# One TensorE loop for all eight attention batches, and VectorE adding all four expert planes: a macaron block on one core

## What is computed

```python
x = x + 0.5 * ffn(layernorm(x))          # mixture of experts + shared expert
x = x + attention(layernorm(x))          # linear attention, causal, 16 heads of 8
x = x + 0.5 * ffn(layernorm(x))          # the same weights as the first

# ffn: scores = softmax(x @ gate_w.T); the top 6 of 64 experts (with gate_b added) take the token
#      y = sum over the 6 of weight * (silu(x @ w1.T) * (x @ w3.T)) @ w2.T   (at most 64 tokens an expert)
#      z = (silu(x @ ws1.T) * (x @ ws3.T)) @ ws2.T                            (every token)
# attention: q = elu(q) + 1, k = elu(k) + 1; out = q.(running sum of k v) / q.(running sum of k)
```

## Time and profile before

| | before |
|---|---|
| median of 3 runs | 602.3 us (601.03 to 602.94) |
| the profiled execution, its own time | 599.64 us |
| its span, first to last instruction | 597.7 us |
| TensorE busy / GpSimd / VectorE / ScalarE | 72% / 55% / 53% / 41% |
| mean granted TensorE clock | 0.716 of full |

### The profile page before, as it was taken

One profiled execution on the slowest core, in us unless ns is written; L12 is line 12 of the kernel. 1 busy time (PEld: TensorE's weight loads), 2 busy tenths in 40 slices (PEclk: granted clock), 3 DMA queues, 4 the chain that ended last, 5 costly groups with the idle time before them and its releaser, 6 DMA issues.

```text
span 597.7 us, 15203 instructions
## 1 busy us (share of the span) xinstructions
PE 427.4 (72%) x5988; PEld 280.2 (47%) x5988; DVE 316.6 (53%) x927; ACT 243.2 (41%) x637; POOL 331.5 (55%) x259
## 2 busy tenths in 40 slices
PE   1884969994689325667999987158676999558970
PEld 1842645552345213455777875156344555224440
DVE  6386982221113992445576763476999322112097
ACT  4872113331223358634577740098411333112420
POOL 6085777888886800311244320005977788887691
PEclk9988785555559855679899985558979555555975
DMA  8997700101008990000021111530000010100592
GB/s 256 379 260 293 286 9 9 10 5 10 6 5 302 409 408 5 0 4 21 18 53 41 48 36 39 202 153 15 0 1 10 7 10 4 10 6 6 202 395 105
DMA packets 34387, 60.38 MB, mean 101 GB/s; under 512 B 12611, under 2 KB 18846, under 8 KB 33870
## 3 DMA queue, kind: packets, MB, share of 16 engines
q1 hardware_dynamic: 23078, 58.41, 27.5%
q0 software_dynamic: 11264, 1.38, 2.6%
HBM read 37.43 MB, written 29.36 MB: 112 GB/s over the span
## 4 chain that ended last, share of the span: by engine, by line
PE 37%; DVE 28%; DMA 13%; issue 11%; POOL 5%; ACT 5%; SPq 1%; POOLq 0%; DVEq 0%; ACTq 0%
DVE X L976 9%; DMA rows_d<-A 5%; PE bank L777 5%; PE upper L877 5%; PE upper L794 4%; DVE Cb L1078 3%; DMA planes_d<-Bb,put_i 3%; ACT A L507 3%; POOL planes_d L438 3%; DVE bn L981 2%; POOL A L452 2%; DMA Bb<-planes_d 2%; PE bank L894 2%; PE upper L913 2%; PE bank L832 2%
## 5 line engine op out<-in xcount | busy, mean ns | idle before, releaser
L438 POOL DMA_INDIRECT planes_d<-Bb,put_i x64 | 100.4, 1569 | 21.5 <-issue 16.0
L479 POOL TENSOR_TENSOR Bb<-Cb,chm 128x576 f32<-128x576 f32 x32 | 36.9, 1183 | 110.3 <-PE upper L924 75.7
L452 POOL DMA_INDIRECT A<-rows_d,tok_i x64 | 71.9, 1124 | 20.6 <-issue 16.9
L1108 DVE TENSOR_TENSOR ring<-ring,bank 128x88 f32<-128x88 f32 x64 | 15.8, 246 | 101.1 <-ACT ring L575 101.1
L674 PE MATMUL bank<-ident,A 128*128 128x128 f32 x96 | 22.5, 412 | 56.4 <-ACT A L507 42.2
L396 POOL TENSOR_TENSOR Bb<-Eb,st 128x512 f32<-128x512 f32 x8 | 8.9, 1115 | 72.4 <-DVE st L1026 72.4
L674 PEld LDWEIGHTS bank<-ident,A 128*128 128x128 f32 x96 | 18.1, 220 | 59.3 <-issue 30.0
L794 PE MATMUL upper<-w2s,ring 88*64 88x128 f32 x256 | 44.0, 448 | 0.0
L1112 DVE TENSOR_SCALAR Bb<-upper,sl 128x128 f32<-128x128 f32 x64 | 22.5, 351 | 30.2 <-PE upper L794 30.0
L976 DVE TENSOR_TENSOR X<-X,A 128x1024 f32<-128x1024 f32 x8 | 18.5, 2318 | 33.9 <-DMA Bb<-planes_d 33.9
L777 PE MATMUL bank<-w1s,ring 128*64 128x88 f32 x256 | 35.6, 378 | 0.0
(11 more groups left out here) (171 smaller groups left out, 1071.3 us busy)
## 6 DMA issues: line engine op xcount, KB each, us to landing
planes_d<-zeros SPq DMA_DIRECT2D x8, 2048.0 KB, 20.7
w3s<-in_w3T SPq DMA_DIRECT2D x2, 2816.0 KB
rows_d<-A SPq DMA_DIRECT2D x8, 512.0 KB, 11.7
A<-planes_d SPq DMA_DIRECT2D x8, 512.0 KB, 9.1
PL<-planes_d SPq DMA_DIRECT2D x8, 512.0 KB, 9.8
Cb<-planes_d SPq DMA_DIRECT2D x8, 512.0 KB, 10.5
Bb<-planes_d SPq DMA_DIRECT2D x8, 512.0 KB, 11.3
w1s<-in_w1T SPq DMA_DIRECT2D x1, 2816.0 KB
```

What stands on the lines that cost most here:

```text
L438: pool.indirect_dma_start(out=planes_d[f], in_=Y[:, s, :], in_offset=None, out_offset=bass.IndirectOffsetOnAxis(ap=put_i[:, s:s + 1], axis=0),
L452: pool.indirect_dma_start(out=A[:, t, :], out_offset=None, in_=rows_d, in_offset=bass.IndirectOffsetOnAxis(ap=tok_i[:, t:t + 1], axis=0), ...
L479: pool.tensor_tensor(out=VX[:, :, :, c, :].rearrange("p q h f -> p (q h) f"), in0=VN.rearrange("p q h f -> p (q h) f"), in1=chm[:, c:c + 1 ...
```

## The change

There are two parts. In attention TensorE's hardware loop runs all eight batches, and no batch is written out. So batch 0 now also runs `turn_out(-1)` and `project_out(-1)` on what lies in the buffers, and batch 7 also runs `project(8)` and `turn_k(8)`; none of these results is used. ScalarE and VectorE raise semaphores in advance or at the end, so that these extra steps find their waits met; their own instructions are the same. In both tails `add_planes` and its semaphore go, and VectorE adds all four planes.

```diff
--- before.py
+++ after.py
@@ gpsimd
-                def add_planes(g):
-                    cols = slice(g * GI * D, (g + 1) * GI * D)
-                    pool.wait_ge(part_in[g], 16 + 64 * (f + 1))
-                    pool.tensor_tensor(out=PLANES[2][:, cols], in0=PLANES[2][:, cols], in1=PLANES[3][:, cols],
-                                       op=ALU.add).then_inc(planes_added, 1)
-
                 for g in range(EARLY, NSH):
-                    if g >= NSH - 2:
-                        add_planes(g - (NSH - 2))
                     shared_gates(g)
-                for g in range(2, NG):
-                    add_planes(g)
@@ scalar
+            act.sem_inc(anT_sb, PRIMED)
...
             def step(b, first=False, last=False):
-                if not last:
+                if last:
+                    act.sem_inc(q_read, 2)
+                    act.sem_inc(k_read, 2)
+                else:
                     features(b + 1)
-                    if not (isinstance(b, int) and b + 2 >= B):
+                    if isinstance(b, int) and b + 2 >= B:
+                        act.sem_inc(hTb_sb, 1)
+                    else:
                         slice_h(b + 2)
@@ tensor
-            for s in (v_ps, sc_ps, kv_ps, pr_ps, o_ps, anT_ps):
+            for s in (v_ps, sc_ps, kv_ps, o_ps):
                 pe.sem_inc(s, PRIMED)
...
-                pe.wait_ge(an_ready, b + 1)
+                pe.wait_ge(an_ready, PRIMED + b + 1)
...
-                pe.wait_ge(anT_sb, b + 1)
+                pe.wait_ge(anT_sb, PRIMED + b + 1)
...
-            def step(b, first=False, last=False):
-                if not last:
-                    project(b + 1)
+            def step(b):
+                project(b + 1)
                 pe.wait_ge(q4_ready, 4 * b + 4)
                 pe.wait_ge(k_ready, PRIMED + b + 1)
-                if not first:
-                    turn_out(b - 1)
+                turn_out(b - 1)
...
-                if not first:
-                    project_out(b - 1)
+                project_out(b - 1)
...
-                if not last:
-                    turn_k(b + 1)
+                turn_k(b + 1)
 
             project(0)
             turn_k(0)
-            step(0, first=True)
-            with pe.Fori(0, B - 2) as i:
-                step(i + 1)
-            step(B - 1, last=True)
+            with pe.Fori(0, B) as b:
+                step(b)
             turn_out(B - 1)
             project_out(B - 1)
@@ vector
-                    for buf in PLANES[0:3]:
-                        if buf is PLANES[2]:
-                            dve.wait_ge(planes_added, NG * (n // 2) + g + 1)
+                    for buf in PLANES:
                         then(dve.tensor_tensor(xg, xg, buf[:, cols], ALU.add))
...
-            for s in (q_ready, k_ready, kv_sb, oo_ready):
+            for s in (q_ready, k_ready, kv_sb, oo_ready, an_ready):
                 dve.sem_inc(s, PRIMED)
...
-                if not last:
+                if last:
+                    dve.sem_inc(k_ready, 1)
+                else:
                     k_feature(b + 1)
```

More of the change, by code:

```diff
@@ L226, in macaron_kernel @@
         z_added = sem("z_added")
-        planes_added = sem("planes_added")
         out_done = sem("out_done")
@@ L885, in step @@
                         pe.wait_ge(v_ready, b + 1)
-                        if not last:
-                            pe.wait_ge(q_read, 2 * (b + 2))
-                            pe.wait_ge(k_read, 2 * (b + 2))
+                        pe.wait_ge(q_read, 2 * (b + 2))
+                        pe.wait_ge(k_read, 2 * (b + 2))
                     for q in AFTER[g]:
@@ L1192, in step @@
                 dve.wait_ge(o_ps, PRIMED + b + 1)
-                if not first:
-                    dve.wait_ge(anT_ps, PRIMED + b)
+                dve.wait_ge(anT_ps, PRIMED + b)
                 ob = upper[:, :, 0:NC * GW].rearrange("p g (n f) -> p g n f", f=E + 1)
```

## The result

| | before | changed |
|---|---|---|
| median | 601.85 us (601.03 to 602.94, 4 runs) | 578.57 us (576.1 to 585.32, 4 runs) |
| ratio | | 0.9598, 95% interval 0.9551 to 0.9646 |
| profiled execution, own time and span | 599.64 and 597.7 us | 577.09 and 575.3 us |

One of the changed kernel's four runs, the one of 585.32, was in a slow state and is left out of the ratio but not of the median above; the median of the other three is 577.09. Five more rounds on another occasion gave 0.9608 (0.9583 to 0.9633). The median fell by 23.3 us (24.8 with the median of the three), where 20.4 were forecast.

What follows compares the result with a forecast made beforehand. No engine bounds the whole: TensorE bounds attention, slowed by code loading and idle time, and VectorE the tails, held by GpSimd. Gains 14.2 + 2.6 + 3.6 = 20.4 us from 602.3 give 581.9, range 577 to 590.

Steps and rivals of the forecast that it cites:

- Batch 0 in the loop: Attention's first pass: still loads code, 19.25 us, plus 1.0 (between 0 and 1.6) for the extra steps.
- Batch 1: Attention's second pass: finds its code in place, so takes 14.19 us like batch 2 before, instead of 19.02.
- batches 2 to 6: Attention's middle passes: 12.63 us each at the full clock, 63.15 together.
- Batch 7 and the end: Attention's last pass in the loop: full clock, no idle time, attention ending at about 361.3 instead of 375.49.
- the first rival: Attention: the clock stays low in batch 7, so attention gives 5.4 + 1.4; time 589.3, chance 0.1.
- a stall behind the loop: Attention's end: code behind the loop may be missing when the branch falls through, costing 0 to 2.8 us.
- the second: Tails give nothing: bunched gates hold VectorE as long as GpSimd's adds did; time 588.1, chance 0.1.
- the third: Attention: each loop pass loads its code again, batches 1 to 7 taking 19 us; time 625.3, chance 0.03.
- the fourth: Attention: code loading was not the issue time, stalls stay in batch 1; time 587.3, chance 0.1.
- The reason given for batch 7: Attention: straight code stops TensorE 1.62 us; 2.71 us idle before ScalarE's k copies brings the clock to 0.59.
- Packets of code: Instruction queue: the changed kernel's trace should show some four to five fewer code packets.
- The tails: Both tails: VectorE no longer held by GpSimd's adds, gaining 2.6 us in stage 0 and 3.6 in the last.

Runs made afterwards that it cites:

- last_straight_full: Changed kernel with TensorE's batch 7 as straight code behind a loop over seven batches, `project(8)` and `turn_k(8)` kept; ratio to before 0.9744.
- loop_only: Kernel before with only the attention loop change, both tails as before; ratio to before 0.9773, median 588.96 us.
- tails_only: Kernel before with only the change to both tails, attention as before; ratio to before 0.9849, median 595.01 us.
- the spare kernels: Changed kernel plus unused GpSimd adds, or memsets of the same size, at the old places; ratios to before 0.9912 and 0.9625.
- after_again: The changed kernel itself, run again as the measure on one chip; 580.29 us, ratio to before 0.9608.
- last_straight: Changed kernel with TensorE's batch 7 as straight code behind the loop, without `project(8)` and `turn_k(8)`; ratio to before 0.9735.
- unrolled: Changed kernel with all eight TensorE batches in straight code, no loop; 613.27 us, ratio to before 1.0262.
- plane_waits: Changed kernel with a semaphore for each plane of each column group; ratio to before 0.9574, and 0.9543 when run again.

## Why the prediction was right

The forecast was 581.9 us in 577 to 590, and 578.57 lies in it. By its own steps:

**Batch 0 in the loop**: 20.2 us forecast, 18.40 measured. I let the added 1.6 us of `turn_out(-1)` and `project_out(-1)` cost 1.0; the batch took 0.85 less than before in spite of them, so the good bound, that they are free, fits. It is not shown: the stretch varies from 17.98 to 19.33 us between the kernels with the loop, which is more than the term. That the extra work hides in the stops for code (0.58, 0.87 and 2.14 us) is the likely reason.

**Batch 1** 14.19 forecast, 14.67 measured; **batches 2 to 6** 63.15 forecast, 63.17 measured. **Batch 7 and the end** 16.1 forecast, 16.48 measured. So attention gave 15.2 where 14.2 stood in the sum. The low clock in batch 7 (the first rival) did not come, nor a stall behind the loop, nor tails that give nothing (the second), nor reloading on each pass (the third), nor stalls left in batch 1 (the fourth).

**The reason given for batch 7** was right in its parts and wrong in their weights. The prediction spoke of a second trouble, the idle 2.71 us and the low clock behind it, and named it beside a stop of 1.62 us for code, as if the larger part were the clock. `last_straight_full` shows the clock kept up and only 1.2 us gained: the two causes overlap, since at the low clock TensorE takes up the time in which it would otherwise wait for code. The change removed both at once, and the sum took batch 7 whole from batch 6, so it did not need the weights and came out right. (The price of the first rival is about 1 us too low: 16.7 - 1.6 + 3 + 5.5 is 23.6 already without the "one more us" for `turn_k(8)`.)

**Packets of code**: "four to five fewer" was wrong, it was eight (27 to 19). I counted one copy of a batch; the change takes away two. `loop_only` has 19 too, and `tails_only` 27.

**The tails**: 2.6 and 3.6 forecast, 4.0 and 5.0 measured. The mechanism and the price of an add (1.22 to 1.23) were right; a gate took 1.26 to 1.40 us by itself, where 1.42 stood. The term mis-sized was the time in which gates hold VectorE. I took 2.8 and 4.2 us. Measured, from the adds above 1.23 us, it is (2.03 - 1.22) + (2.18 - 1.22) = 1.8 in the tail of stage 0, where the last gate ran beside the statistics. In the last tail three adds are held, and not one for a gate's full 1.4 us:

```profile
550.27 2.17 DVE L961 TENSOR_TENSOR X<-X,PL 128x1024 f32<-128x1024 f32 x1
...
553.74 2.17 DVE L961 TENSOR_TENSOR X<-X,Bb 128x1024 f32<-128x1024 f32 x1
...
556.02 2.09 DVE L961 TENSOR_TENSOR X<-X,A 128x1024 f32<-128x1024 f32 x1
```

That is 0.95 + 0.95 + 0.87 = 2.8 us. GpSimd beside them shows why a held add costs less than a gate:

```profile
549.06 2.30 POOL L420 TENSOR_TENSOR w3s<-w3s 88x512 f32<-88x512 f32 x1 [0.45 <-ACT w3s L536]
...
555.14 1.89 POOL L420 TENSOR_TENSOR w3s<-w3s 88x512 f32<-88x512 f32 x1 [0.32 <-ACT w3s L536]
```

Both gates start beside an add of VectorE and are held themselves: they end 1.12 us after it (550.24 to 551.36, 555.91 to 557.03). The next add ends 1.08 us after the gate. So the two do not overlap, and behind a gate the add needs 1.08 us where it takes 1.22 alone; a held add costs VectorE 0.9 to 1.0 us, not 1.4. One bound in the sum was too kind as well: the prediction says itself that all four gates in the way would leave the last tail 2 us, and then adds up the low side with 3.6. With 2 it comes to 589, still inside the stated range.

**What no step foresaw**: 1.1 us ahead of `project(1)`. `loop_only`, the spare kernels and `after_again` have 21.0 to 21.3 us there, while `tails_only`, `last_straight`, `last_straight_full`, `unrolled` and both runs of `plane_waits` have 22.1 to 22.2. So every trace with the short stretch has the loop over eight batches, and of the kernels with that loop only `plane_waits` has the long one: it may well belong to the change, though the loop starts only behind this stretch. In the changed kernel the clock rises within the first projection (L827 takes 1.51 us and L829 1.05), in the kernel before it does not (1.91 both). What decides it I did not test. The stretch from the last projection to the last tail varies from 190.9 to 194.9 us and the one ahead of the first tail from 187.9 to 192.0 (both without `plane_waits`), as much as a tail gives.
